# GpSimd gathers adapter rows before it stores weight sums; adapter units in banks of their own; residual and A_down rows fetched later

## The reference, cut to what matters

```python
def _L1_cond_ref(x, W_gate, ...):          # B, N, H, F = 32, 64, 1024, 2752; 16 adapters of rank 16
    gate = lora_add(einsum('bnh,fh->bnf', x, W_gate), x, A_gate, B_gate)
    up   = lora_add(einsum('bnh,fh->bnf', x, W_up), x, A_up, B_up)
    act  = silu(gate) * up
    return lora_add(einsum('bnf,hf->bnh', act, W_down), act, A_down, B_down)

x = x + einsum('bct,bcd->bdt', x, L0_weights[itok_0])            # layer 0
x = x + _L1_cond_ref(x, ...)                                     # layer 1, adapters by itok_1
x = x + (irfft(rfft(x) * rfft(K)) + x * D) * mask_of_lengths     # layer 2, K from S4D parameters
x = x + einsum('bct,bcd->bdt', x, L3_weights[itok_3]) + bias     # layer 3
```

## Time and profile before

| what | value |
|---|---|
| median of 3 runs | 1781.54 us (1781.05 to 1784.63) |
| profiled execution | 1782.16 us, its span 1780.7 us |
| TensorE matmul / weight load busy | 94% / 80% |
| VectorE, ScalarE, GpSimd busy | 71%, 40%, 21% |
| DMA | 313.75 MB, mean 176 GB/s |

### The profile page before, as it was taken

The page is one execution under the profiler, slowest core; times in us unless marked ns, Lnnn a source line. Parts: engine busy times, 40 slices in busy tenths (PEclk is TensorE's granted clock), DMA queues, the critical chain, the costliest instruction groups (busy, mean ns, idle before and its releaser), DMA issues.

```text
span 1780.7 us, 27132 instructions
## 1 busy us (share of the span) xinstructions
PE 1667.6 (94%) x8664; PEld 1422.4 (80%) x8664; DVE 1256.3 (71%) x1881; ACT 706.8 (40%) x1075; POOL 379.8 (21%) x445
## 2 busy tenths in 40 slices
PE   6788999999999799999899999999998999989998
PEld 6777777777777787888788888888887777879997
DVE  4866667766667486855677777777766988758887
ACT  4333333333333254433233333333333453336656
POOL 6231222211222101012022222222212000253230
PEclk9899999999999899999999999999999999999999
DMA  8554454344453589867333333333335758676754
GB/s 252 184 147 136 154 162 154 120 140 147 155 162 130 189 279 312 267 217 261 117 113 117 115 106 116 117 106 118 115 111 208 247 191 276 217 255 239 242 168 190
DMA packets 148090, 313.75 MB, mean 176 GB/s; under 512 B 18242, under 2 KB 42978, under 8 KB 146754
## 3 DMA queue, kind: packets, MB, share of 16 engines
q1 hardware_dynamic: 110578, 218.17, 37.4%
q0 software_dynamic: 20176, 63.43, 11.2%
q10 hardware_dynamic: 17280, 31.46, 4.7%
HBM read 249.78 MB, written 69.50 MB: 179 GB/s over the span
## 4 chain that ended last, share of the span: by engine, by line
PE 49%; DVE 7%; DMA 5%; issue 2%; POOL 2%; ACT 1%; SPq 1%; another core or an unknown queue 0%; DVEq 0%; ACTq 0%
PE ps L1150 34%; PE ps L1419 5%; DMA ysub<-act_dram 4%; PE ps L1416 3%; DVE dhl L1910 2%; PE ps L1190 2%; POOL wbd L658 2%; PE ps L1448 1%; DMA draw<-in_bd,row_d 1%; DVE draw L1922 1%; PE ps L1432 1%; PE ps L1163 1%; PE ps L1231 1%; PE ps L1229 1%; ACT dhl L839 1%
## 5 line engine op out<-in xcount | busy, mean ns | idle before, releaser
L1150 PE MATMUL ps<-xop,aop_a 128*128 128x512 f32 x2016 | 472.7, 390 | 0.0
L1150 PEld LDWEIGHTS ps<-xop,aop_a 128*128 128x128 f32 x2016 | 372.9, 188 | 73.9
L1150 PE MATMUL ps<-xop,aop_b 128*128 128x512 f32 x1512 | 371.6, 395 | 42.8 <-DVE t L1864 35.6
L1150 PE MATMUL ps<-dhl 128*128 128x512 f32 x1680 | 389.6, 392 | 14.5 <-DVE dhl L1910 13.1
L1150 PEld LDWEIGHTS ps<-dhl 128*128 128x128 f32 x1680 | 314.3, 188 | 86.5 <-DVE dhl L1910 20.0
L1150 PEld LDWEIGHTS ps<-xop,aop_b 128*128 128x128 f32 x1512 | 278.2, 189 | 108.2 <-issue 48.8
L839 ACT ACTIVATE dhl<-draw 128x1024 fp32r<-128x1024 f32 x156 | 164.6, 1059 | 264.9 <-PE ps L1150 149.6
L1910 DVE TENSOR_TENSOR dhl<-draw,dhl 128x1024 fp32r<-128x1024 f32 x156 | 189.4, 1220 | 64.0 <-ACT dhl L839 63.5
L658 POOL DMA_INDIRECT lb_raw<-in_bgu,row_b x168 | 179.2, 1066 | 74.8 <-issue 38.6
L1852 DVE TENSOR_TENSOR lb_hl<-lb_raw,lb_hl 128x1024 fp32r<-128x1024 f32 x42 | 51.5, 1225 | 124.4 <-ACT lb_hl L839 124.4
L1824 DVE TENSOR_TENSOR aop_b<-raw,aop_b 128x512 fp32r<-128x512 f32 x84 | 58.0, 691 | 75.9 <-ACT aop_b L839 75.8
(11 more groups left out here) (240 smaller groups left out, 2247.4 us busy)
## 6 DMA issues: line engine op xcount, KB each, us to landing
raw<-in_wgu SPq DMA_DIRECT2D x168, 256.0 KB, 4.0
draw<-act_dram SPq DMA_DIRECT2D x140, 256.0 KB
rtoep<-k_dram SPq DMA_DIRECT2D x64, 512.0 KB, 4.6
draw<-ws_dram SPq DMA_DIRECT2D x80, 256.0 KB
draw<-in_wd SPq DMA_DIRECT2D x76, 256.0 KB
ysub<-act_dram SPq DMA_DIRECT2D x60, 256.0 KB
wsum<-in_wds SPq DMA_DIRECT2D x20, 512.0 KB, 5.4
act_dram<-t ACTq DMA_DIRECT2D x40, 256.0 KB
```

The lines of the kernel that those rows point to most:

```text
L1150: ins = pe.matmul(bank, wt, r, start=start and k == 0 and n == 0, stop=stop and k == nk - 1 and n == 2, skip_group_check=True)
```

## The change

GpSimd's loop gathers first and stores the sums of the weights of two iterations ago afterwards; the last store follows the gathers of `wbd`. The A_down gathers of pass 1 are taken out of the opening and done in iterations 4 to 7, four in each. Each of the four adapter units has a bank of its own, and TensorE no longer waits for `t_unit` before units 2 and 3; the bank groups of the down product are changed to suit. ScalarE and VectorE split units 2 and 3 ahead of the `lr` rows, `t_unit` and `rest`; the split of the first A_down rows comes after `rest_silu(1)` and `rest_out(1)`. `residual_in` waits for every second step (24, 26, 28, 30 in pass 0) and begins at step 21 instead of 6 in pass 1. ScalarE waits for the last store before it overwrites `xraw`.

```diff
-BANKS = ((6, 7, 0, 1), (2, 3, 4, 5))
+BANKS = ((6, 7, 2, 3), (0, 1, 4, 5))
...
-        TGB = (6, 3)
-        REST_BANK = ((0, 5), (2, 5))
+        UNIT_BANK = ((6, 7, 2, 3), (0, 4, 6, 7))
+        REST_BANK = ((0, 5), (1, 5))
...
             load_lb(0, 0)
             pool.wait_ge(ad_gathered, 16 * 2 * CB)
-            gather_ads(1)
             pool.dma_start(len_i[:, :], length.partition_broadcast(P)).then_inc(par_in, 16)
+
+            def store_sums(v):
+                pool.wait_ge(ws_sum, 4 * (v + 1))
+                pool.dma_start(ws_dram[v], wsum[:, 1:5, :]).then_inc(ws_stored, 16)
+
             for f in range(1, NF):
                 load_lb(0, f)
-
-                pool.wait_ge(ws_sum, 4 * f)
-                pool.dma_start(ws_dram[f - 1], wsum[:, 1:5, :]).then_inc(ws_stored, 16)
+                if f > 1:
+                    store_sums(f - 2)
+                if 4 <= f < 8:
+
+                    gather_ads(1, *divmod(f - 4, 2))
             pool.wait_ge(prod, n_f(0, NF - 1, PER_F) + 1)
             for n in range(NQ):
                 rows_of(wbd1[:, n, :], w0[:, :], row_w[:, NQ + n:NQ + n + 1], w0_in[NQ])
+            store_sums(NF - 2)
...
             def residual_in(p, at):
...
-                        pool.wait_ge(d_lo, n_lo(p, at + i))
+                        pool.wait_ge(d_lo, n_lo(p, at + 2 * i))
...
-            residual_in(1, 6)
+            residual_in(1, 21)
...
@@ ScalarE, pass_
+                for kh in range(2):
+                    unit_hi(p, 2, kh)
                 lr_split(p)
                 for kh in range(2):
-                    unit_hi(p, 2, kh)
+                    unit_hi(p, 3, kh)
+                rest_silu(p, 0)
                 if first:
                     form_hi(0, 4)
-                rest_silu(p, 0)
-                for kh in range(2):
-                    unit_hi(p, 3, kh)
                 act.wait_ge(w_used, p * USED_PASS + 8)
                 a_split(p, 0, Q1)
                 a_split(p, 0, Q6)
-                if first:
-                    form_hi(0, 5)
-                xraw_free(act, p)
-                ad_split(p, -1, None)
                 act.wait_ge(w_used, p * USED_PASS + 9)
                 a_split(p, 0, Q5)
                 a_split(p, 0, Q7)
+                if first:
+                    form_hi(0, 5)
                 rest_silu(p, 1)
+                xraw_free(act, p)
+                ad_split(p, -1, None)
...
                 if first:
+
+                    act.wait_ge(ws_stored, 16 * LEFT)
                     for q in range(NQ):
                         l0_copy(1, q)
...
@@ TensorE, unit, free_banks and pass_
-                if u >= 2:
-                    pe.wait_ge(t_step, p * T_STEPS + 3 * (u - 2) + 1)
                 cols = slice(half * HT, half * HT + HT)
-                bank = ps[:, TGB[p] + half, 0:HT]
+                bank = ps[:, UNIT_BANK[p][u], 0:HT]
...
-                        pe.wait_ge(l0_copied, NQ + (5, 5, 7, 7)[j])
+                        pe.wait_ge(l0_copied, NQ + (5, 5, 6, 6)[j])
                     elif j >= 2:
-                        pe.wait_ge(ev, n_ev(p, NF) - 1)
+                        pe.wait_ge(ev, n_ev(p, NF) - 3)
...
                 pe.wait_ge(x_lo, p * NPROD + 4)
+                if p:
+                    pe.wait_ge(d_ev, n_evd(0, 9, 0))
                 unit(p, 2)
...
@@ VectorE, pass_ (t_unit reads UNIT_BANK too)
+                for kh in range(2):
+                    unit_lo(p, 2, kh)
                 t_unit(p, 0)
+                t_unit(p, 1)
                 lr_lo_part(p)
                 for kh in range(2):
-                    unit_lo(p, 2, kh)
-                t_unit(p, 1)
+                    unit_lo(p, 3, kh)
                 if first:
                     t4_raw(p)
+                rest_out(p, 0)
+                if first:
                     form_lo(p, 4)
-                rest_out(p, 0)
-                for kh in range(2):
-                    unit_lo(p, 3, kh)
                 t_unit(p, 2)
+                t_unit(p, 3)
                 sums(p, 0)
                 a_low(p, 0, Q1)
                 a_low(p, 0, Q6)
-                t_unit(p, 3)
+                a_low(p, 0, Q5)
+                a_low(p, 0, Q7)
                 if first:
                     t3_raw(p)
                     form_lo(p, 5)
+                rest_out(p, 1)
                 ad_low(p, -1, None)
-                a_low(p, 0, Q5)
-                a_low(p, 0, Q7)
-                rest_out(p, 1)
```

14 lines of the change are left out of this document (7 added, 7 removed).

## The result

The changed kernel takes 1723.61 us (median of 4: 1719.32, 1722.64, 1724.58, 1724.91), against 1781.3 for the kernel before: a ratio of 0.9669, 95% interval 0.9647 to 0.9691. A later set of five executions gave 1726.03 and 0.9677 (0.9664 to 0.9691). The forecast was 1709, its own range 1701 to 1716, the range over all rivals 1699 to 1724: the direction and the largest term are right, but the median is 15 us above the forecast, outside its own range, and inside the wide one by 0.4 us. That it fell inside is luck as much as skill; the numbers nearest to it are those of rivals A (1722) and B (1724). The forecast change was 72 us (from 1781 to 1709), the measured one is 58.

A forecast was written before the change was run, and what follows sets the result against it. Bound: TensorE idling in pass 0's frames behind a store-gather-split ring. Terms -47.6 -7.7 -7.5 -4.9 -1.3 -7.5 +2.0 +0.5 = -74.0 gave 1707.5, taken as 1709 us (chance 0.60); own range 1701 to 1716, all rivals 1699 to 1724.

The forecast's parts named there:

- rivals A: Residual's stall moves to steps 21 to 27, both adapter gathers late, with lower clock once or twice: 1722, chance 0.14.
- Rival B: Frames: SyncE's queue binds, raw blocks land over 8 us after issue, t late, 0.8 us a frame: 1724, chance 0.08.
- The ring: Pass 0 frames: store, gather, landing, split, t, wsum, store, 24.31 us around; cutting it gives 21.95 a frame, -47.6.
- each of the four iterations with four adapter gathers ... Nothing: Pass 0 frames: about 7 us of gathers end 4.3 us into the next frame, before lb_lo at 6: no cost.
- the replay: Opening of pass 0 retimed in the new order: frame 1 starts at 98.4 instead of 106.12, -7.7 (-2.8 to -12).
- End of pass 0: Frame 20 to down product: TensorE's 8.15 us wait for wbd goes, down product starts earlier: -7.5 (-4.5 to -9.5).
- The step that put draw 1 at 23 us into the frame: End of pass 0: ScalarE's split of draw 1 at 23 instead of 25.5 us, lb gather out of the backlog.
- Step 31 of pass 0: Down product: adapter gather issued about 8 us later behind residual loads, so TensorE starts the step late: +2.0 (0 to +4.5).
- The residual in pass 1: Down product: loads moved to steps without ysub, draws keep half of 405 GB/s, stall goes: -7.5 (0 to -8.7).
- the later theory: Written for the early, half-pace run, not the prediction: small backlog covered by four steps' look-ahead, down product 237 to 240 us.
- The bank term: Pass 1: banks 2 and 3 are free before banks 0 and 1 were, a wait of 1.35 us: -1.3.
- The best case: Lower limit of the range for all: everything would have to go best, -82.8, below 1699.

The follow-up runs named there:

- the early one: Changed kernel with pass 1's residual begun at step 6 instead of 21, still one load every second step: 1731.79 us, one run.
- the late burst: Changed kernel with pass 1's residual from step 21 at one load every step instead of every second: 1724.28 us, one run.

## Why the prediction was right, and where it was not

**Frames of pass 0: right in mechanism, one burst missed.** The ring was the cause and cutting it is worth 47.7 (forecast 47.6 with the gathers' half microsecond in it). What the changed kernel lost against that, 4.5 us, comes from the step "each of the four iterations with four adapter gathers ... Nothing". I weighed whether GpSimd would be late for lb_lo (it isn't) and forgot that the same gathers share the DMA engines with the raw blocks: VectorE waits 2.63 us for a raw block at 179.28, and TensorE is idle for 3.5 us in those four frames; with the gathers one a frame it is idle for nothing. Rival B was this wait, but in all 19 frames; it came in four.

**Opening of pass 0: -5.3 for -7.7.** The first half of the replay holds: unit 2 at 47.64 (said 47.4), gap 2.37 (2.2), unit 3 at 54.47 with none (54.3). It drifts by 1.2 at frame 0 (69.19 for 68.0; it waits for a split of VectorE, which I had not in the list) and by as much again in it: the gap before the third product is 5.17 (3 to 4) and that product runs 5.23 us for 2.9, at the lower clock. I had written "maybe with the lower clock" and not priced it. The gap that was to shrink to 3 to 4 us is as long as before (5.19).

**End of pass 0 and opening of pass 1: right in size, the first with luck.** -7.2 for -7.5, -5.0 for -4.9; the wait for wbd is gone, unit 3 has no gap. Over the six executions the first is -5.9. The step that put draw 1 at 23 us into the frame failed: ScalarE's split of it starts at 24.6 (547.45; 25.5 before), and the executions of this code lie at 24.3 to 25.6.

**Step 31 of pass 0: +6.8 for +2.0, the mis-sized term.** The gather's issue was 9.4 us later in the product (86.6 for 77.2; I said 8), its landing 4.6 (92.3 for 87.7), and TensorE started the step 4.6 us later than before (94.71 for 90.12), the high end of my bound. Behind it came what this term left out (rival A had it, at 1.7 us): the gap of 5.14 us takes the clock down, the 16 matmuls last 1.6 us longer, and the granted clock of the first 3.55 us is 0.50, 1.2 of 2.4 GHz; from there to the end the product takes 2.2 us more than before (133.23 for 130.98). By the estimate from the Trainium skill, "DMA: Bandwidth & Descriptors", section "Anatomy of one DMA", the term was near +1.5; the trace does not agree, nor with my +2.0. The gather follows the residual through the same queue, and that most likely sets its landing: the last load was issued 10.3 us later in the product than before and landed 5.2 us later (91.0 for 85.8), the gather 1.3 us behind it.

**The residual in pass 1: right in size, with one step of the reason wrong.** -9.2 for -7.5 - 1.3 + 0.5 = -8.3 (over seven executions -7.2). I weighed what the loads need, 191 GB/s late and 287 with `ysub`, against half of 405, and both experiments come out as that weighing says: early at half pace stalls, late at full pace doesn't. (What fell with the early one was the later theory, which had left `ysub` out.) But the half is wrong. The rule of the Trainium skill that a DMA engine alternates between the queues that have work ("DMA: Bandwidth & Descriptors", "Queues, rings and completion order") is told there for packets, and the trace agrees with that and not with equal bytes. In the kernel before, in the very stretch of the earlier trace rows that gave 405 GB/s:

```profile
q0 software_dynamic: 804, 2.96, 74.2%
q1 hardware_dynamic: 819, 1.09, 29.8%
```

The packets are nearly equal in number (804 and 819), but the residual's hold 3.7 KB and the others' 1.3 KB, so SyncE's queue moved 109 GB/s in these 10 us (1370 to 1380) and not 202. The prediction's sentence that no run shows the split is thus wrong, too: this trace had it. By 109 the draws of the late place, with their 191, would have had to fall behind as well; they did in the late burst (96 GB/s), and it cost nothing. The most likely reason is the four steps of look-ahead, which the prediction did not use. The bank term in it (-1.3) is worth -0.5.

**What the sum hid.** The terms' misses are -4.4, -2.4, -4.8 on one side and +0.9 on the other, so its own mechanisms at their measured size give 1719 where the sum said 1708; the median lies 4 us higher still, as the profiled execution was the fastest. I had said that the replays were "more likely too good" and had moved the forecast by 1.5 us for it (1707.5 to 1709). Rival A's second half (adapter gather late, with the lower clock behind it) is what happened in pass 0, without its first; B's wait happened in four frames. Neither is the case to which 0.60 was given. The best case was also added up short: the best ends of the terms give -84.6, not -82.8.

## What to carry to other kernels

When work is moved on an engine that issues DMAs, ask two questions: who waits for the moved instruction, and whose transfers it will now run beside. 16 gathers in bursts of four cost 4.5 us, and nothing at one a frame. Where loads are held back by a consumer two steps behind them, moving the burst away gained some 10 us here and halving its pace only 3; a deeper buffer was not tried. Before giving a queue its share of the engines, read the shares by queue in a trace: equal packets are not equal bytes. Look also at what stands ahead on the same queue: here the indirect gather landed behind the residual loads issued before it each time. And price a TensorE gap of some 5 us with what follows it: here the gap of 5.14 cost 2.2 us more in lower clock, and one of 1.07 nothing.
